# Second mixture of experts: half tiles of 64 rows, two experts in column tiles per step, outputs scattered into tables and summed by TensorE

## What is computed

```python
w, sel = _routing(x, gate_w)          # softmax weights of the top 4 of 32 experts, normalised
def _moe(x2d, Wg, Wu, Wd, cw):
    g = jnp.einsum('th,ehi->eti', x2d, Wg)
    u = jnp.einsum('th,ehi->eti', x2d, Wu)
    a = jax.nn.silu(g) * u * cw.T[:, :, None]
    return jnp.einsum('eti,eih->th', a, Wd)
large = _moe(x, Wg, Wu, Wd, cw_large)      # 32 experts, inner width 96
small = _moe(x, cWg, cWu, cWd, cw_small)   # 16 experts, inner width 128, each for a pair of the 32
return (large + SMALL_SCALE * small).reshape(B, S, H)
x = _layernorm(x + _L1_ffn_ref(...), axis=-1)
```

## Time and profile before

| | us |
|---|---|
| median of 3 runs | 1425.54 |
| lowest and highest | 1423.03 to 1430.25 |
| the profiled execution | 1424.44 |
| its span by the profile | 1422.6 |
| PE busy in the span | 1207.9 (85%) |
| VectorE busy | 879.4 (62%) |
| ScalarE busy | 557.8 (39%) |
| GpSimd busy | 526.6 (37%) |

### The profile page before, as it was taken

How to read it: one execution, slowest core, us unless ns; L and a number is a source line. 1 busy time by engine, 2 the same in 40 slices (tenths; PEclk the granted TensorE clock), 3 DMA queues, 4 the chain that set the end, 5 groups by cost and what they waited for, 6 DMA issues and landing times.

```text
span 1422.6 us, 21890 instructions
## 1 busy us (share of the span) xinstructions
PE 1207.9 (85%) x7065; PEld 810.8 (57%) x7071; DVE 879.4 (62%) x2197; ACT 557.8 (39%) x1460; POOL 526.6 (37%) x616
## 2 busy tenths in 40 slices
PE   7688998999878859899999989999999509888881
PEld 3554664677743437566775356633677407777770
DVE  1678886753597992857637877587774533444443
ACT  2247776885351101366400167512773302222210
POOL 2253773643143221445400034300443362444444
PEclk9899999999968979899979999999999758999996
DMA  7165995000001001100030000002203523555544
GB/s 292 45 225 161 320 327 169 17 1 1 30 1 44 1 0 75 57 4 2 2 126 1 0 0 2 1 1 85 123 1 119 205 102 70 83 81 84 85 62 107
DMA packets 69614, 110.73 MB, mean 78 GB/s; under 512 B 5057, under 2 KB 59841, under 8 KB 66241
## 3 DMA queue, kind: packets, MB, share of 16 engines
q1 hardware_dynamic: 58896, 96.62, 20.1%
q0 software_dynamic: 10608, 12.72, 6.2%
HBM read 57.41 MB, written 51.91 MB: 77 GB/s over the span
## 4 chain that ended last, share of the span: by engine, by line
PE 64%; DVE 16%; DMA 6%; issue 6%; POOL 5%; ACT 2%; SPq 1%; POOLq 0%; DVEq 0%; ACTq 0%
PE ps L701 8%; PE ps L690 6%; PE ps L979 6%; PE ps L710 4%; PE ps L682 4%; DMA sums<-mem 3%; PE ps L683 3%; PE ps L1033 2%; PE ps L960 2%; PE ps L650 2%; PE ps L812 2%; PE ps L1030 2%; DMA mem<-slots 2%; POOL mem L1837 2%; PE ps L864 2%
## 5 line engine op out<-in xcount | busy, mean ns | idle before, releaser
L1837 POOL TENSOR_SCALAR mem<-mem 128x512 f32<-128x512 f32 x256 | 177.5, 698 | 386.4 <-DVE mem L1172 383.2
L1167 DVE TENSOR_REDUCE mem<-ps 128x1 f32<-128x512 f32 x256 | 175.3, 687 | 107.9 <-PE ps L683 99.5
L1663 ACT ACTIVATE mem<-ps,mem 128x512 f32<-128x512 f32 x256 | 177.0, 695 | 13.3 <-DVE mem L1167 12.6
L690 PE MATMUL ps<-mem 128*128 128x128 f32 x1024 | 159.3, 279 | 13.5 <-POOL mem L1837 12.6
L690 PEld LDWEIGHTS ps<-mem 128*128 128x128 f32 x1024 | 118.6, 141 | 68.4 <-POOL mem L1837 49.7
L1656 ACT ACTIVATE mem<-ps 128x512 f32<-128x512 f32 x192 | 115.9, 605 | 91.5 <-PE ps L690 91.0
L1893 POOL DMA_INDIRECT sums<-mem x63 | 97.1, 1541 | 131.6 <-DVE mem L1525 111.1
L682 PE MATMUL ps<-rounded_at 128*128 128x512 f32 x256 | 124.4, 486 | 11.7 <-DVE rounded_at L1156 10.4
L701 PE MATMUL ps<-mem 128*64 128x256 f32 x1024 | 125.5, 387 | 2.4 <-ACT mem L1656 2.4
L1847 POOL TENSOR_TENSOR mem<-mem 128x512 f32<-128x512 f32 x40 | 55.4, 1384 | 139.1 <-DVE mem L1208 139.0
L1631 ACT ACTIVATE rounded_at<-ps 64x512 fp32r<-64x512 f32 x64 | 37.8, 591 | 165.6 <-PE ps L962 153.0
(11 more groups left out here) (255 smaller groups left out, 2476.2 us busy)
## 6 DMA issues: line engine op xcount, KB each, us to landing
slots<-mem SPq DMA_DIRECT2D x15, 2312.0 KB, 10.4
mem<-in_f_w_dram SPq DMA_DIRECT2D x16, 1024.0 KB, 9.2
mem<-slots SPq DMA_DIRECT2D x63, 136.0 KB, 2.5
mem<-in_f_w_dram SPq DMA_DIRECT2D x24, 256.0 KB, 3.3
mem<-in_x_wq_dram SPq DMA_DIRECT2D x2, 2048.0 KB, 13.3
mem<-in_x_wo_dram SPq DMA_DIRECT2D x2, 2048.0 KB, 8.4
mem<-sums SPq DMA_DIRECT2D x8, 256.0 KB, 4.4
mem<-in_x_wqr_dram SPq DMA_DIRECT2D x1, 1536.0 KB, 6.7
```

The costliest lines, as they stand in the source:

```text
L690: mm = pe.transpose(ps[3 + j % 2][:, k * P:(k + 1) * P], PR[j % 6][:, k * P:(k + 1) * P], ident)
L1167: dve.tensor_reduce(nmax[:, i % 8:i % 8 + 1], ps[SB[lay][i % len(SB[lay])]][:, :], AX.X, ALU.max, negate=True)\
L1663: act.activation(PR[i % 6], ps[SB[lay][i % len(SB[lay])]][:, :], ACT.Exp, bias=nmax[:, i % 8:i % 8 + 1], accum_out=esum[:, i % 8:i % 8 + 1 ...
L1837: pool.tensor_scalar(PR[i % 6], PR[i % 6], rinv[:, i % 8:i % 8 + 1], 1.0, ALU.mult, ALU.mult)\
```

## The change

Experts are cut into half tiles of 64 rows: at most 95, so 96 slots (`SLOTS`) and 48 steps (`STEPS`) of two. Half tile 2i is in the partitions 0 to 63 of step i, half tile 2i+1 in 64 to 127, usually of different experts. SP makes two loads of 64 rows a step and refills the ring when PE has turned step i-8 and VectorE has its weights. The matmuls of gates and down are issued twice, with 64 columns of the stationary operand and to one half of the PSUM partitions each: the first expert's weights by an address from a register, as before, the second's from `WB`, a ring of three copies. ScalarE makes the copy (`weights_copied`): it reads the two addresses into registers and copies 640 and 768 values a partition.

PE's order in a step n is now rows_turned(n+1), acts_turned(n-1), gates(n), down(n-1).

The rows in `slots` carry four destinations (token + 1024 x (k+1)) in place of the index. VectorE picks weight and destination together (`weight_of`: three instructions for two), unused rows get a spare destination. GpSimd scatters the weighted rows without adding into `parts`, which has one table of 1024 rows for each of the four choices and a spare one; no scatter waits for another. At the end SP loads all four tables (16 DMAs of 256 KB for 8), PE sums residual and four tables in PSUM by multiplying with the identity (`parts_summed`), and VectorE's statistics and normalisation read PSUM. The residual is no longer stored, and `sums` needs no clearing.

```diff
-K1, TILES = 4, 63
+K1, HALF = 4, 64
+SLOTS, STEPS = 96, 48
...
-            for t in range(NT):
-                sp.wait_ge(xn_ready, 4 * NT + t + 1)
-                sp.dma_start(sums[0][t * P:(t + 1) * P, :], X[:, t, :]).then_inc(s_keep, 16)
             sp.wait_ge(s_scat, 16 * NT * K1)
             sp.wait_ge(e_tabs, 1)
-            for i in range(TILES):
+            for i in range(STEPS):
                 if i >= 8:
-                    sp.wait_ge(s_add[i % 2], 16 * ((i - 8) // 2 + 1))
+                    sp.wait_ge(e_xt, i - 7)
+                    sp.wait_ge(e_w, i - 7)
                 if i >= 4:
-                    sp.wait_ge(row_ld[i % 4], 16 * (i // 4))
-                row = sp.value_load(where[0:1, 2, i:i + 1], min_val=0, max_val=DUMMY * P)
-                sp.dma_start(rows1[:, i % 8, :], slots[bass.ds(row, P), :]).then_inc(row_ld[i % 4], 16)
-            for k in range(2):
-                sp.wait_ge(s_add[k], 16 * ((TILES + 1 - k) // 2))
+                    sp.wait_ge(row_ld[i % 4], 32 * (i // 4))
+                for h in range(2):
+                    row = sp.value_load(where[0:1, 2, 2 * i + h:2 * i + h + 1], min_val=0, max_val=DUMMY * P)
+                    sp.dma_start(rows1[HALF * h:HALF * h + HALF, i % 8, :], slots[bass.ds(row, HALF), :]).then_inc(row_ld[i % 4], 16)
+            for i in range(8):
+                sp.wait_ge(s_put[i], 16 * STEPS // 8)
             for q in range(NT // 2):
-                for k in range(2):
-                    sp.dma_start(R[k][:, 2 * q:2 * q + 2, :], blocks_of(sums[k])[:, 2 * q:2 * q + 2, :]).then_inc(s_back[q // 2], 16)
+                for j in range(K1):
+                    sp.dma_start(R[j][:, 2 * q:2 * q + 2, :], blocks_of(parts)[:, NT * (j + 1) + 2 * q:NT * (j + 1) + 2 * q + 2, :]).then_inc(s_back[q], 16)
...
                     pe.wait_ge(e_xte, i + 1)
+                    pe.wait_ge(e_wb, i + 1)
                     if i >= 2:
                         pe.wait_ge(e_a, i - 1)
                     both = ps[2 + i % 2][:, 0:448].rearrange("p (a n) -> p a n", a=2)
                     for c in range(DC):
-                        pe.matmul(both[:, :, 0:I1], xT1[:, i % 2, c, :], mem[:, bass.ds(at_large[i] + 2 * I1 * c, 2 * I1)],
+                        pe.matmul(both[0:HALF, :, 0:I1], xT1[:, i % 2, c, 0:HALF], mem[:, bass.ds(at_large[i] + 2 * I1 * c, 2 * I1)],
+                                  start=c == 0, stop=c == DC - 1)
+                        pe.matmul(both[HALF:P, :, 0:I1], xT1[:, i % 2, c, HALF:P], WB[i % 3][:, 2 * I1 * c:2 * I1 * (c + 1)],
                                   start=c == 0, stop=c == DC - 1)
...
                 rows_turned(0)
-                for n in range(TILES + 2):
-                    if n + 1 < TILES:
+                for n in range(STEPS + 1):
+                    if n + 1 < STEPS:
                         rows_turned(n + 1)
-                    if n < TILES:
+                    if n >= 1:
+                        acts_turned(n - 1)
+                    if n < STEPS:
                         gates(n)
-                    if 1 <= n <= TILES:
-                        acts_turned(n - 1)
-                    if n >= 2:
-                        down(n - 2)
+                    if n >= 1:
+                        down(n - 1)
+
+            def parts_summed():
+                pe.wait_ge(e_y, STEPS)
+                for t in range(NT):
+                    pe.matmul(ps[t][:, 0:D], ident, X[:, t, :], start=True, stop=False)
+                for t in range(NT):
+                    pe.wait_ge(s_back[t // 2], 16 * K1)
+                    for j in range(K1):
+                        mm = pe.matmul(ps[t][:, 0:D], ident, R[j][:, t, :], start=False, stop=j == K1 - 1)
+                    mm.then_inc(y_added, 1)
...
+                def weights_copied(i):
+                    large = act.value_load(where[0:1, 0, 2 * i + 1:2 * i + 2], min_val=72 * 256, max_val=200 * 256 - 640)
+                    small = act.value_load(where[0:1, 1, 2 * i + 1:2 * i + 2], min_val=72 * 256, max_val=200 * 256 - 768)
+                    weights_loaded(act, i)
+                    if i == 1:
+                        act.wait_ge(s_scat, 16 * NT * K1)
+                    if i >= 3:
+                        act.wait_ge(e_dn, i - 2)
+                    n = 4 * I1 + D
+                    act.activation(WB[i % 3][:, 0:n], mem[:, bass.ds(large, n)], ACT.Copy)
+                    act.activation(WB[i % 3][:, n:], mem[:, bass.ds(small, 4 * IC1 + D)], ACT.Copy).then_inc(e_wb, 1)
...
-                    pool.indirect_dma_start(sums[i % 2], bass.IndirectOffsetOnAxis(ap=rows1[:, i % 8, IDX:IDX + 1].bitcast(U32), axis=0),
-                                            y1[:, i % 4, :], None, bounds_check=B * S + P - 1, oob_is_err=True,
-                                            compute_op=ALU.add).then_inc(s_add[i % 2], 16)
+                    pool.indirect_dma_start(parts, bass.IndirectOffsetOnAxis(ap=goal[:, i % 8:i % 8 + 1].bitcast(U32), axis=0),
+                                            y1[:, i % 8, :], None, bounds_check=(K1 + 1) * B * S - 1, oob_is_err=True).then_inc(s_put[i % 8], 16)
```

More of the change, by code:

```diff
@@ L328, in program, with weights_loaded @@
         counts, tiles_of, start_of, end_of, shift_of = (at(61 + 0.125 * i, 1) for i in range(5))
-        from_start, from_end, inside = (at(62 + 0.25 * i, 64) for i in range(3))
-        table = at(63, 4 * 64, pattern="p (k i) -> p k i", k=4)
-        R = [at(kb, NT * D, pattern="p (t d) -> p t d", t=NT) for kb in (48, 56)]
+        from_start, from_end, inside = (at(62 + 0.375 * i, SLOTS) for i in range(3))
+        table = at(63.25, 4 * SLOTS, pattern="p (k i) -> p k i", k=4)
+        R = [at(72 + 8 * j, NT * D, pattern="p (t d) -> p t d", t=NT) for j in range(K1)]
         RB = [6, 7, 0, 1]
         block = ctx.enter_context(nc.Block())
+        def weights_loaded(eng, i):
+            chunk = min(i, len(CHUNK_KB) - 1)
+            if chunk < EARLY:
+                eng.wait_ge(w_early, 16 * EARLY)
+            elif chunk < MIDDLE:
+                eng.wait_ge(w_middle, 16 * (MIDDLE - EARLY))
+            else:
+                eng.wait_ge(w_late, 16 * (len(CHUNK_KB) - MIDDLE))
         def folded(k, copy):
@@ L999, in dispatch_layer1 @@
                 pe.wait_ge(e_rhs, 1)
-                pe.matmul(ps[3][:, 0:256], ones[0:E1, :], table[0:E1, :, :].rearrange("p k i -> p (k i)"), start=True,
+                pe.matmul(ps[3][:, 0:4 * SLOTS], ones[0:E1, :], table[0:E1, :, :].rearrange("p k i -> p (k i)"), start=True,
                           stop=True).then_inc(e_tab, 1)
@@ L1488, in tables_layer1 @@
                 dve.wait_ge(e_tab, 1)
[L1489 to L1490 removed]
+                for h in range(2):
+                    r = slice(HALF * h, HALF * h + HALF)
+                    dve.tensor_copy(of_tile[r, :], ps[3][r, 2 * SLOTS + h:3 * SLOTS:2])
+                dve.tensor_scalar(where[:, 0:2, :], ps[3][:, 0:2 * SLOTS].rearrange("p (k i) -> p k i", k=2), 1.0, float(CHUNK_KB[0] * 256),
                                   ALU.mult, ALU.add)
[L1492 removed]
+                dve.tensor_scalar(where[:, 2, :], ps[3][:, 3 * SLOTS:4 * SLOTS], float(HALF), float(DUMMY * P), ALU.mult, ALU.add).then_inc(e_tabs, 1)
             def experts_layer1():
```

135 lines of the change are left out of this document (66 added, 69 removed).

## The result

The changed kernel takes 1430.89 us (median of 20 runs, 1428.36 to 1436.97) against 1424.97 us for the kernel before (20 runs). The ratio is 1.0038, with a 95% interval of 1.0025 to 1.0051. A second comparison, beside later runs of the kernel before, gave 1.0040 (1.0017 to 1.0063; one of those runs of the kernel before took 1638.83 us in the chip's slow state and is left out). So it is slower by some 5.5 us, 0.4%, which 20 runs a side resolve but which lies inside the half per cent that the prediction counts as no change. The profiled execution took 1429.75 us, with a span of 1427.9.

The account below looks back on a forecast made before the run. It took PE to bound most of the stage now, and a chain through address reads after the change. Stage +6.9 and tail +0.3 us give 1425.5 + 7.2, about 1433 us; range 1414 to 1460.

Parts of the forecast that it names:

- the half per cent: Whole kernel: a time within 0.5%, 7 us, of the kernel before counts as no change; chance 0.31.
- The chain decides: Each expert step: PE's sequencer stops at the activations, so reads, gates, silu and activations run in series, 4.46 us.
- Rival B, the reads run ahead: PE's address reads pass the waiting transposes and are hidden; step about 3.65 us, 38 us less, 1395; chance 0.11.
- ScalarE just fits: ScalarE in each step: reads and weight copies done at 6.05 us, before the silu is due at 6.28; costs nothing.
- Rival D, ScalarE as the bound: ScalarE's reads and copies take 1 us more than summed, step 0.5 longer, 23 us: 1456; chance 0.11.
- Packing: Gates and down: both half-tile matmuls run at once, a pair costing what one costs now, plus 0.16 us per mode change.
- Rival E: Half-tile pairs run one after the other; gates take 1.5 us more a step, 71 us: 1504; chance 0.03.
- Ring and loads: SP's row loads: waits for scatters go, but the first gates need four loads and start 2.2 us later.
- Clock: Expert stage: starts at 1.2 GHz, three slow steps of 1.5 us each extra, then no fall.
- rival C: Gaps in the steps make PE's clock fall; one slow step in three adds 26 us: 1459; chance 0.11.
- Stage: Expert steps to the last weighting: ends at 1398.6 against 1391.74 us, +6.9, the late first gates included.
- Tail: Last weighting to program end: PE's sum of four tables replaces VectorE's additions, +0.3 us in all.

Follow-up runs that it names:

- gates-first run: Changed kernel with TensorE's and ScalarE's address reads early, plus gates ahead of activation transposes and down two steps late: 1383.23 us, ratio 0.9740.

## Why the prediction was right, and where it wasn't

The forecast was 1433 us, within 1414 to 1460, and the median is 1430.89; the sign (slower) is right, though the result lies just within the half per cent, to which I gave 0.31 rather than the 0.54 of slower.

*The chain decides.* Right, and shown twice: the order alone turned 3.38 us a step into 4.24 in the kernel before, and moving the reads turned 4.32 into 3.42 in the changed one. Link by link: reads to first gates 1.67 + 0.05 forecast, 1.61 measured from the first read; gates to silu 1.82, measured 1.78; silu to activations 0.85 and 0.85; to TensorE 0.07, measured 0.05. The step is 4.32 us (mean) to 4.46 forecast. The first link was forecast 0.11 too long, its allowance of 0.05 for one more semaphore included; the second 0.04, out of an allowance of 0.1. Over 47 steps the 0.14 make 6.6 us.

*Rival B, the reads run ahead.* Refuted as a description of this kernel; its price was near: where TensorE's reads do run ahead, 39 us go (38 forecast, with a step of 3.65, where 3.42 was measured), and with ScalarE's too 56. The Trainium skill (TensorE: Matmul & The Clock Gate, opening table) lists a queue of 64 instructions for TensorE, behind which one would expect the reads to hide. The rows show that they hide only as long as the sequencer is not standing at a semaphore; 64 us of issue in the stage are the difference.

*ScalarE just fits.* Right: copies end 0.35 us before the silu, forecast 0.23. The copies take 1.47 us in sum to 1.5 forecast (0.64 from start to start, then 0.83), though the 0.605 us row that the estimate used reads PSUM, not SBUF as it says. Its reads I took at 1.5 behind the row copy; they start with the copy and leave 0.85 us of idle time behind it. Leaving the copies out gave nothing. Rival D, ScalarE as the bound, is refuted for the changed kernel; it holds in the one with TensorE's reads early.

*Packing.* Right: pairs start 10 ns apart, sixteen passes of the gates take 1.56 us. The price of a change of mode, 0.16 forecast from L701, is 0.14. That it is hidden in the changed kernel but not behind a full TensorE is what the gates-first run adds. Rival E is refuted: the pairs never ran one after the other.

*Ring and loads.* The ring's waits went, as forecast. That the scatter-add in them was worth 20 us was in the sum as part of the 3.46 us per tile, without a price of its own. The first gates came 2.6 us later to 2.2 forecast.

*Clock.* No fall in the stage: rival C is refuted with a share of 1.00 from 1187 to 1385 us. Cold steps I took at 4.5 us in all; last gates minus first gates minus 47 x 4.32 gives 1.2 and 3.1 us in the two profiles.

*Stage.* Forecast +4.4 us from first gates to last weighting; against the two profiles of before, which themselves differ by 3.4, it is -5.5 to -0.2. This is the term that was mis-sized, by the 0.14 us a step and the cold steps.

*Tail.* Forecast +0.3 us to the last statistics, measured +0.3 in the first pair of profiles and up to 2.6 with the others, since the sum's cold stretch differs: 15.9 and 17.0 us to 16.3 forecast. What I missed is the drain: "behind it 5.9 + 0.2 as now" took the end of the program as fixed, and it grew by 2.5 us. So that the total came out within 3 us is partly luck: a stage that was forecast too long and an end that was forecast too short stand against each other. The profiled execution of after besides held a pause of VectorE that the second one didn't have.

## What to carry to other kernels

In these runs an address read into a register was free only while its engine's sequencer was ahead of the array. Put it in front of the last wait, not behind it: here two lines moved on each of two engines turned a kernel 0.4% slower into one 3.5% faster. When the order of calls is changed, follow each call's register reads, not only its matmuls, and put work of one array mode side by side. Where a forecast sums parts of a program, take the closing drain of each engine as one of the parts.

## What the runs showed of the hardware that I had not expected

- TensorE runs two column halves beside each other even where all matmuls of one product's first half stand ahead of those of its second in the program; that costs 0.13 us a step.
- Each change between full width and column halves costs 0.14 us, visible as later starts on both sides of it.
- GpSimd's drain at the end of the program lasts 4.73 us behind 32 plain scatters and 63 scatter-adds, 7.22 behind 80 plain ones, 8.45 behind 95. Semaphores and waits don't change it. Why a plain scatter weighs more there than an add stays open.
- A step without ScalarE's copies is longer (4.46 us to 4.32) than one with them.
- An fp32 matmul with the identity takes two passes where the transpose takes one (0.43 us to 0.22 for a pair of 128 columns each).
- VectorE stood still for 13.8 us in one of 14 profiled executions: the step of a semaphore that TensorE raises is recorded 14.6 us behind the end of its matmul, and GpSimd's scatters came 4 us later for it. The reason isn't in the trace.
